# 256-channel deformable stages: the first group's table tiles for the second block two taps later, its shifted offset product one tap later

## The reference, cut to what matters

```python
h = relu(group_norm(x, gn1_g, gn1_b))
h = deform_conv(h, dw1, pw1, pwb1, w1, b1)
h = relu(group_norm(h, gn2_g, gn2_b))
h = deform_conv(h, dw2, pw2, pwb2, w2, b2)
return h + x

def deform_conv(x, dw, pw, pwb, w, b):
    f   = depthwise 7x7 conv(x, dw)            # per channel
    off = 1x1 conv(f, pw) + pwb                # 18 values a pixel: y and x of 9 taps
    py, px = pixel + tap + off                 # sampling points
    sampled = bilinear_gather(x, py, px)       # 4 corners, weighted
    return einsum('bckhw,ock->bohw', sampled, w) + b
```

## Time and profile before

| | |
|---|---|
| median of three runs | 5544.22 us (5543.78 to 5546.28) |
| the profiled execution | 5542.41 us, span of its records 5540.6 us |
| PE busy | 5014.1 us, 90% of the span |
| DVE busy | 4109.8 us, 74% |
| ACT busy | 2300.3 us, 42% |
| POOL busy | 3214.2 us, 58% |
| DMA | 812.32 MB, mean 147 GB/s |
| the four 256-channel stages, by ACT's first instruction | 3673.1, 4166.3, 4654.4 and 5139.6 us |

### The profile page before, as it was taken

The page is one execution under the profiler, slowest core; times in us unless marked ns, Lnnn a source line. Parts: engine busy times, 40 slices in busy tenths (PEclk is TensorE's granted clock), DMA queues, the critical chain, the costliest instruction groups (busy, mean ns, idle before and its releaser), DMA issues. The chain is left out here.

```text
span 5540.6 us, 75123 instructions
## 1 busy us (share of the span) xinstructions
PE 5014.1 (90%) x23052; PEld 2327.8 (42%) x23052; DVE 4109.8 (74%) x6738; ACT 2300.3 (42%) x4176; POOL 3214.2 (58%) x2823
## 2 busy tenths in 40 slices
PE   7999999999799999999978869969987996999688
PEld 3333333333333333333336656745543553555344
DVE  4888888885488888888533334458987896888898
ACT  2444444443244444444311111125544554555455
POOL 0666666665066666666527757746645663665676
PEclk9999999999899999999968879979998998999899
DMA  2000000000100000000034435559988998999999
GB/s 73 1 1 1 1 1 1 1 1 5 58 1 1 1 1 1 1 1 1 2 101 122 128 106 159 165 212 374 370 321 309 388 373 305 381 383 359 386 410 359
DMA packets 320277, 812.32 MB, mean 147 GB/s; under 512 B 70094, under 2 KB 137556, under 8 KB 319758
## 3 DMA queue, kind: packets, MB, share of 16 engines
q0 software_dynamic: 193536, 679.59, 32.6%
q1 hardware_dynamic: 126478, 129.39, 6.8%
HBM read 708.40 MB, written 100.43 MB: 146 GB/s over the span
## 5 line engine op out<-in xcount | busy, mean ns | idle before, releaser
L645 POOL TENSOR_TENSOR arena<-arena 128x512 f32<-128x512 f32 x960 | 1419.0, 1478 | 790.9 <-ACT arena L1274 726.4
L1274 ACT ACTIVATE arena<-ps 128x1024 f32<-128x1024 f32 x1024 | 1049.5, 1025 | 1215.7 <-PE ps L823 1186.3
L1797 DVE TENSOR_REDUCE arena<-ps 128x2 f32<-128x1024 f32 x1024 | 1244.8, 1216 | 387.5 <-PE ps L797 387.5
L697 POOL DMA_INDIRECT arena<-corners,arena x1152 | 1099.2, 954 | 684.1 <-issue 316.3
L2027 DVE SCALAR_TENSOR_TENSOR ps<-arena,ps 128x256 f32<-128x256 f32 x2304 | 956.0, 483 | 232.1 <-DVEq L2021 223.5
L1146 PE MATMUL ps<-arena 128*128 128x512 f32 x2304 | 1046.5, 597 | 0.2
L823 PE MATMUL ps<-arena 64*128 64x512 f32 x4096 | 1046.0, 589 | 0.0
L836 PE MATMUL ps<-arena 128*64 128x512 f32 x4096 | 991.3, 605 | 0.0
L1819 DVE TENSOR_TENSOR arena<-arena 128x512 f32<-128x512 f32 x960 | 830.9, 865 | 62.7 <-ACT arena L1274 62.1
L681 POOL DMA_INDIRECT arena<-corners,arena x576 | 546.6, 949 | 277.6 <-issue 246.2
L1459 ACT ACTIVATE ps<-arena 128x256 f32<-128x256 f32 x1152 | 499.7, 469 | 469.3 <-DMA arena<-corners,arena 203.3
(11 more groups left out here) (163 smaller groups left out, 3717.0 us busy)
## 6 DMA issues: line engine op xcount, KB each, us to landing
corners<-arena SPq DMA_DIRECT2D x256, 256.0 KB
arena<-corners,arena POOLq DMA_INDIRECT x1728, 8.9
img<-in_x SPq DMA_DIRECT2D x8, 1024.0 KB, 9.4
corners<-arena SPq DMA_DIRECT2D x128, 64.0 KB, 2.2
arena<-in_wd SPq DMA_DIRECT2D x2, 2304.0 KB, 8.4
between<-img SPq DMA_DIRECT2D x4, 1024.0 KB, 6.3
arena<-between SPq DMA_DIRECT2D x4, 1024.0 KB, 8.8
resid<-img SPq DMA_DIRECT2D x8, 512.0 KB
```

The costliest lines, as they stand in the source:

```text
L645: pool.tensor_tensor(SUMS[u % 2][:, 0, :], SUMS[u % 2][:, 0, :], P[n % 4][:, 0, :], ALU.add).then_inc(sum_a, 1)
L697: pool.indirect_dma_start(G3[4 * k + t].rearrange("p a c -> p (a c)"), None, table256[b], bass.IndirectOffsetOnAxis(ap=IS3[:, k, t:t + 1], ...
L1274: af(P[n % 4].rearrange("p h q -> p (h q)"), ps[:, 2 * (n % 2):2 * (n % 2) + 2, :].rearrange("p h q -> p (h q)"), ACT.Exp, scale=float(D) ...
L1797: v.tensor_reduce(mxp[u % 2][:, :, t, j], ps[:, 4:6, :], AX.X, ALU.max).then_inc(mx_done, 1)
```

## The change

In the first group alone, the two table parts of block 1 move on PE from k = 0 and 1 to k = 2 and 3, their copies on ACT from k = 1 and 2 to k = 3 and 4, and the shifted offset product on PE from k = 4 to k = 5. The first group is told apart by a new argument `first`. Nothing is added or removed, and the fourth stage, which has no side slot, is not touched.

```diff
+                def beside(n, k, first, ahead, last):
+
+                    begins = 2 if first else 0
+                    if begins <= k <= begins + 1 and not last:
+                        side_table3(k - begins)
                     if k == 2:
                         side_shifts_done()
                         if ahead:
                             side_normal_done(CH)
-                    if k == 4:
+                    if k == (5 if first else 4):
                         side_shifted(T3[0], 7, O3, sel3_s)
...
-                nine(0)
+                nine(0, first=True)
...
                     if k < 2 and ahead:
                         side_normal(side, n + 2, k)
-                    begins = 1 if first else 2
+                    begins = 3 if first else 2
                     if begins <= k <= begins + 1 and not last:
                         side_copy3(k - begins)
```

More of the change, by code:

```diff
@@ L1152, in tap, with staged_tap @@
                         last.then_inc(st_free, 1)
-                def staged_tap(g, k, ahead, last):
+                def staged_tap(g, k, first, ahead, last):
                     pe.wait_ge(st_ready, CH)
@@ L1160, in staged_tap @@
                     if side is not None:
-                        beside(g, k, ahead, last)
+                        beside(g, k, first, ahead, last)
                     tap(g, k)
-                def beside(n, k, ahead, last):
-                    if k < 2 and not last:
-                        side_table3(k)
+                def beside(n, k, first, ahead, last):
+                    begins = 2 if first else 0
+                    if begins <= k <= begins + 1 and not last:
+                        side_table3(k - begins)
                     if k == 2:
@@ L1175, in beside, with nine @@
                         side_rows3(side, n + 1, range(2 * (k - 2), 2 * (k - 1)))
-                def nine(g, ahead=True, last=False):
+                def nine(g, first=False, ahead=True, last=False):
                     for k in range(KK):
-                        staged_tap(g, k, ahead, last)
+                        staged_tap(g, k, first, ahead, last)
                 if side is not None:
```

## The result

The changed kernel takes 5516.25 us, median of five runs (5511.19 to 5521.61), against 5544.22 us. The ratio is 0.9947, 95% interval 0.9932 to 0.9962. The forecast was 5511, and the range 5503 to 5524. The profiled execution took 5511.57 us, 30.84 less than the one before (5542.41); the forecast for it was 5509.5.

A forecast was written before the change was run, and what follows sets the result against it. PE was taken to bound the groups. Stage gains of 12.0, 11.3 and 12.0 us sum to 35.3; 5542.41 - 35.3 + 2.4 for the clock = 5509.5, and the median 1.8 us higher gives 5511, range 5503 to 5524.

The forecast's parts named there:

- PE sets the pace, and what the opening gains is kept: Full groups: PE busy 52.98 of 55.00 us, so a stage keeps its opening's gain if PE holds that pace.
- step 1: First stage's opening: DVE runs taps 2 and 3 straight after its shifts, 4.71 us each, from 3699.85 to 3709.3.
- step 3: First copy of block 1: block 0's writes are in by 3709.6, no delay from the longer gather queue.
- Rival B: Block 0's writes come late behind two more gathered taps, leaving about 2 us a stage: 5538; chance 0.04.
- step 6: First group: two taps gained at PE's pace of 6.01 us each, 12.0 us in the first stage.
- The clock: TensorE in the stage openings: pauses cost 2.4 us in one of the two stages with the longer pause.
- Rival E: TensorE's clock falls in all three openings, costing 4.4 us a stage: 5522; chance 0.10.
- The wait on `ts_free0` falls under 3 us: ACT's waits before the table copy, summed over three stages, fall from 41.6 us to under 3.
- The data keeps up: First group's gathers: taps arrive in time, with DVE some 5 us to spare at tap 10.
- rival A: Data sets the first group's pace, so only 8 us a stage is gained, 24 us: 5520; chance 0.08.
- The shifted product is free: PE in the first group: moved product done by about 3733, before DVE wants it at 3734.7, at no cost.
- The forecast's own range: Whole kernel: 5503 (no clock loss, one or two slow openings gone) to 5517 (half of Rival E's clock loss).

The follow-up runs named there:

- rows_early: Changed kernel with the first group's rows product for block 1 one turn earlier, partly ahead of tap 2's transposes; 5507.0 us, 0.9931 of the kernel before.
- lag2_rows_warm: lag2_rows plus two matmuls that compute nothing needed between the halves of tap 2's transposes; 5500.5 us, 0.9923 of the kernel before.
- delay1: Changed kernel with table parts and copies one tap later than originally instead of two, shifted product at k = 4; 5522.5 us, 0.9957 of the kernel before.
- warm: Changed kernel with five matmuls that compute nothing needed filling PE's two pauses around tap 2's transposes; 5509.9 us, 0.9930 of the kernel before.
- lag2_rows: Changed kernel with ACT's copies at k = 4 and 5 and block 1's rows product one turn earlier; 5496.15 us, 0.9909 of the kernel before.
- shift_at4: Changed kernel with the first group's shifted offset product back at k = 4; 5511.7 us, 0.9939 of the kernel before.
- change_again: The changed kernel unaltered, measured once more on the chip of the next three kernels; 5519.7 us, 0.9949 of the kernel before.
- warm_tr: As warm, but PE's two pauses filled with 24 and 16 transposes instead of five matmuls; 5505.2 us, 0.9929 of the kernel before.

## Why the prediction was right, and where it was off

- *PE sets the pace, and what the opening gains is kept*: right for the change. Groups 1 to 5 take 54.9 to 55.0 us, or a slow opening's 56.7, and no gain was given back. rows_early and lag2_rows_warm show where it ends: there PE came to group 1 before DVE, and part or all of the gain was lost.
- *Taps 2 and 3 run from the end of the shifts* (step 1): right, 4.70 us each, without a pause.
- *The writes end when they did* (step 3): right. The hardware queue's last packet of block 0 ended 36.6, 36.6 and 37.0 us into the three stages, against 36.1, 35.7 and 36.8 before, with two more taps behind the gathers in flight. delay1 shows the same, with one more tap, by a copy that does wait for them. Rival B falls.
- *One tap gained is one tap of PE's pace* (step 6): right, by delay1 for one tap (16.0 us in three stages, where 18 would be in full). For two taps 35.3 us was the sum at full clock, and warm, which has the full clock in all three openings, gives 281.6 - 247.1 = 34.5.
- *The clock*: the term that was mis-sized. I took 2.4 us in one of two stages. It fell in all three stages, in this profile and in the second, and cost 2.5 + 1.7 + 2.7 = 6.9 us at the first copy, and 5.2 in the second profile. warm gives back 7.1 and 5.3 us. Rival E had the mechanism right, but its 4.4 us a stage was too dear, since the clock rose again within the product and part of the loss lay beside DVE's tap 3. What I had weighed wrongly was the evidence. I took the opening of group 2, which kept the clock, as a likeness of these openings, though its pauses are 0.33 and 1.70 us and theirs are 2.1 to 3.5 and 1.2 to 1.7.
- *The wait on `ts_free0` falls under 3 us*: the profile has 17.3 us in three waits by that name, but the writes were done 3.0 to 4.4 us before each of them ended, so PE ended them. The prediction had noted that the wait may be put down to PE; it came out the other way about, and a wait for PE was put down to the writes. Some 11 of the 17.3 us are the wait for PE at full clock, which the prediction had at 3 to 5 us a copy (in warm the same waits are 3.66, 3.76 and 3.85), and the rest is the clock.
- *The data keeps up* (against rival A): right. In the first group of stage 1 ACT waits for a gather twice, 1.36 and 2.03 us, both beside PE's work. lag2_rows goes another 19 us faster through the three first groups with the same data.
- *The shifted product is free*: right, by shift_at4.
- *The forecast's own range*: its ends do not follow from the terms. Without a clock loss the sum gives 5542.4 - 35.3 + 1.8 = 5508.9, and one or two slow openings fewer make it 5505.5 to 5507.2, not 5503. With half of rival E's loss it gives 5515.5, not 5517. The measured median, 5516.25, lies 0.7 us above that.

The first groups gave 27.4 us where 35.3 - 2.4 = 32.9 were forecast. That the profiled execution is still within 2.1 us of the forecast is luck: the groups behind were 2.9 us shorter, mostly by two slow openings fewer, and stage 1 began 1.35 us earlier, less the 0.9 us of the fourth stage. I can claim none of these. The medians carry less of it: they are 28.0 and, in change_again, 25.3 us below the kernel before, where 33 were forecast, and the first of them stands 5.2 us above the forecast. What stays open is why the start of stage 1 lies up to 12 us apart from one profile to the next. The traces say where it comes from: up to 2450 us ACT's same instructions lie within some 3 us of each other in six of these profiles, and they part between 2450 and 2860 us and again near 3250, in the layers ahead. Which wait does it was not followed, and no run here was aimed at it.

## What to carry to other kernels

An in-order engine that waits for a slow transfer makes everything behind it wait, and moving work that doesn't need the transfer ahead of that wait pays at the pace of the engine that bounds the stage, one unit of work for each unit moved. Ask next what the engines then wait for in the new place: here it was TensorE at half clock, after pauses no longer than 3.5 us that the change itself had left. Filling the pauses gives that back only if the next place where TensorE waits doesn't lose it again, as in lag2_rows_warm. A wait in this profile had the name of the last wait in the code, not of the one that ended last, so look at when the named transfer really ended.

## What the runs showed of the hardware

- Two DMA queues with work moved packet for packet, 1 KB elements against 4 KB rows (535 and 538 packets in 6 us). With two more taps in the gather queue the writes ended at most 0.9 us later (after: 36.6, 36.6 and 37.0 us into the stages; change_again: 36.0, 36.1 and 37.0; before: 36.1, 35.7 and 36.8).
- TensorE's clock fell to 1.2 GHz in all six first-group openings of the changed kernel in two profiles. PE had two pauses there, of 2.1 to 3.5 us and of 1.2 to 1.7 us, with four transposes between. It stayed at 2.4 GHz in the six of warm and warm_tr, where these pauses were filled, but for at most 1.2 us, with matmuls or with float32 transposes (in the first stage of warm_tr 5.2 us of transposes alone).
- With shorter pauses it did either. At group 1's opening, with 0.25 and 1.7 us, it stayed up in stage 1 of one profile of the changed kernel and fell in the other (55.0 and 56.7 us for the group). With 1.2 and 1.7 us it stayed up in stage 3 of lag2_rows and fell in stage 3 of rows_early and of lag2_rows_warm.
